# A macaron block of MoE FFN and Mamba: the FFN down projection as three f32r products, with its weight halves streamed

## The reference

```python
x = x + 0.5 * ffn(layernorm(x))        # call f1
x = x + attn(layernorm(x))             # Mamba block and gated MLP
x = x + 0.5 * ffn(layernorm(x))        # call f2, same weights

def ffn(x):                            # 32 experts of 96, top 6, shared 192
    scores = sigmoid(x @ gate_w); topk_w, topk_i = top_k(scores, 6)
    combine = one-hot sum of topk_w / sum(topk_w)
    act = silu(einsum('td,edf->tef', x, wg)) * einsum('td,edf->tef', x, wu)
    routed = einsum('tef,efd,te->td', act, wd, combine)
    return routed + (silu(x @ sg) * (x @ su)) @ sd

def attn(h):                           # d_inner 512, 16 states, conv 4
    h = h + mamba(rmsnorm(h))
    return h + mlp(rmsnorm(h))         # gated MLP, 1024 hidden
```

## Time and profile before

| | us |
|---|---|
| median of 3 runs | 1938.59 (1936.56 to 1942.36) |
| the profiled execution, its own time | 1936.02 |
| its span in the profile | 1934.2 |
| PE busy (matmuls) | 1601.1 (83%) |
| DVE busy | 1295.1 (67%) |
| POOL busy | 720.2 (37%) |
| ACT busy | 705.1 (36%) |

### The profile page before, as it was taken

How to read it: one execution, slowest core, us unless ns; L and a number is a source line. 1 busy time by engine, 2 the same in 40 slices (tenths; PEclk the granted TensorE clock), 3 DMA queues, 4 the chain that set the end, 5 groups by cost and what they waited for, 6 DMA issues and landing times. The chain is left out here.

```text
span 1934.2 us, 25234 instructions
## 1 busy us (share of the span) xinstructions
PE 1601.1 (83%) x7512; PEld 1194.2 (62%) x7512; DVE 1295.1 (67%) x2331; ACT 705.1 (36%) x1418; POOL 720.2 (37%) x838
## 2 busy tenths in 40 slices
PE   6776768677978988789888989788988998678999
PEld 5665557555755557455664557555675567556888
DVE  3236984688468964789466974689648974896343
ACT  4234424433352425333343423433244334432211
POOL 4411552244134532345223542245324542353222
PEclk9887889878999999899998999899999999988999
DMA  7752223323232222222231223222232223323563
GB/s 260 281 170 91 86 86 99 111 88 98 78 106 72 81 89 74 105 74 80 80 104 65 84 77 95 85 77 88 81 98 93 87 77 86 126 88 101 174 205 133
DMA packets 72751, 204.77 MB, mean 106 GB/s; under 512 B 12928, under 2 KB 22368, under 8 KB 72224
## 3 DMA queue, kind: packets, MB, share of 16 engines
q1 hardware_dynamic: 64416, 177.86, 27.7%
q0 software_dynamic: 8192, 25.17, 4.5%
HBM read 179.39 MB, written 15.73 MB: 101 GB/s over the span
## 5 line engine op out<-in xcount | busy, mean ns | idle before, releaser
L595 PE MATMUL gub<-x_hi,wr 128*128 128x256 f32 (+1 forms) x1144 | 460.5, 403 | 83.5 <-DVE hid L963 60.6
L675 PE MATMUL acc<-hid,w_down 128*128 128x256 f32 (+1 forms) x1144 | 423.9, 498 | 0.9 <-DVE hid L963 0.8
L1218 POOL TENSOR_TENSOR hid<-hid,weight 128x256 f32<-128x256 f32 (+1 forms) x264 | 263.5, 998 | 428.0 <-DVE hid L963 409.9
L824 ACT ACTIVATE hid<-gub 128x256 f32<-128x256 f32 (+1 forms) x350 | 160.9, 460 | 680.5 <-PE gub L597 590.5
L596 PE MATMUL gub<-x_lo,wr 128*128 128x256 f32 (+1 forms) x1144 | 395.7, 346 | 0.0
L597 PE MATMUL gub<-x_hi,wr 128*128 128x256 f32 (+1 forms) x1144 | 394.7, 345 | 0.0
L1231 POOL TENSOR_TENSOR ring<-ring 128x512 f32<-128x512 f32 x192 | 245.8, 1280 | 314.4 <-DVE ring L1118 314.4
L1112 DVE TENSOR_TENSOR_SCAN ring<-decays,side 128x512 f32<-128x512 f32 x256 | 310.7, 1214 | 4.1 <-DVE side L1103 1.5
L595 PEld LDWEIGHTS gub<-x_hi,wr 128*128 128x128 f32 x1144 | 231.9, 203 | 122.1 <-issue 73.9
L675 PEld LDWEIGHTS acc<-hid,w_down 128*128 128x128 f32 x1144 | 212.9, 201 | 88.3 <-issue 68.8
L596 PEld LDWEIGHTS gub<-x_lo,wr 128*128 128x128 f32 x1144 | 232.3, 203 | 21.1 <-issue 4.3
(11 more groups left out here) (115 smaller groups left out, 1725.4 us busy)
## 6 DMA issues: line engine op xcount, KB each, us to landing
wr<-w_halves SPq DMA_DIRECT2D x260, 512.0 KB, 3.3
wm_gu<-in_w_mlp POOLq DMA_DIRECT2D x64, 256.0 KB, 3.0
w_halves<-wr SPq DMA_DIRECT2D x26, 512.0 KB, 4.9
wm_down<-in_w_mlp POOLq DMA_DIRECT2D x64, 128.0 KB, 2.6
w_raw<-in_w_gu SPq DMA_DIRECT2D x26, 256.0 KB, 4.7
cst<-decays SPq DMA_DIRECT2D x192, 32.0 KB, 1.9
xin<-in_x SPq DMA_DIRECT2D x8, 256.0 KB, 3.4
x<-in_x SPq DMA_DIRECT2D x8, 256.0 KB, 2.6
```

The costliest lines, as they stand in the source:

```text
L595: mm(out, w[:, 0, half, k, :], x_hi[:, k, a:b], start=(k == 0), stop=False)
L675: last = mm(acc[k][:, a:b], w, h[:, a:b], start=(c == 0), stop=(c == (MLP_CHUNKS if mlp else FFN_CHUNKS) - 1))
L824: A(hid[c % HSLOTS][:, a:b], s.gub_of(it)[:, a:b], ACT.Tanh, scale=0.5).then_inc(sem["tanh_done"], 1)
L1218: nc.gpsimd.tensor_tensor(h, h, weight[c // 3 % CSLOTS][:, a:b], ALU.mult).then_inc(sem["weighted"], 1)
```

## The change

The down projection becomes three f32r products per output half, as gate and up are: high weights times high hidden values, high times low, low times high. For this the hidden values are split in a new item `hh`: ACT copies hid to f32r (`h_hi`), POOL subtracts (`h_lo`), four slots each. The down weights are no longer resident: each chunk's raw tile, weight slot and DRAM copy hold gate, up and down. In turn 0 the subtraction of `ws` moves from POOL to DVE. DLAG goes from 3 to 4, a weight slot is freed by `down` instead of `u`, and the reload items move to the position of that down. The diff, cut to its core:

```diff
-WSLOTS, MSLOTS, HSLOTS = 8, 3, 4
+WSLOTS, MSLOTS, HSLOTS, PSLOTS = 8, 3, 4, 4
...
+    "hh": {"hid_hi": 1, "hid_lo": 1},
...
-DLAG = 3
+DLAG = 4
...
+        out += [("hh", "ff", p - 2)] if 2 <= p <= FFN_CHUNKS + 1 else []
         out += [("down", "ff", p - DLAG)] if p >= DLAG else []
         out += [("by_g", "ff", p), ("u", "ff", p)] if now else []
+        used = p - DLAG
         if splits:
             out += [("keep_w", p)] if now else []
             out += [("raw", p + RAWS)] if p + RAWS < FFN_CHUNKS else []
             out += [("ws", p + WAHEAD)] if p + WAHEAD < FFN_CHUNKS else []
-        elif p + WSLOTS < FFN_CHUNKS:
-            out += [("wl", p + WSLOTS)]
-        if now and more and p == last_in(p % WSLOTS):
-            out += [("wln", p % WSLOTS)]
+        elif used >= 0 and used + WSLOTS < FFN_CHUNKS:
+            out += [("wl", used + WSLOTS)]
+        if more and used >= 0 and used == last_in(used % WSLOTS):
+            out += [("wln", used % WSLOTS)]
...
-        w_raw = [sb(f"w_raw{i}", [P, 2, KC, P]) for i in range(RAWS)]
-        w_down = sb("w_down", [P, FFN_CHUNKS, DM])
+        w_raw = [sb(f"w_raw{i}", [P, 3, KC, P]) for i in range(RAWS)]
...
-        wr = [sb(f"wr{i}", [P, 2, 2, KC, P], F32R) for i in range(WSLOTS)]
+        wr = [sb(f"wr{i}", [P, 2, 3, KC, P], F32R) for i in range(WSLOTS)]
...
+        h_hi = [sb(f"h_hi{i}", [P, 2 * SEQ], F32R) for i in range(PSLOTS)]
+        h_lo = [sb(f"h_lo{i}", [P, 2 * SEQ], F32R) for i in range(PSLOTS)]
...
-                    sp.dma_start(w_raw[c % RAWS][:], d["w_gu"][c]).then_inc(sem[f"w_raw{c % RAWS}"], 16)
-                    for i, (lo, hi) in enumerate(SLICES):
-                        if c == max(lo, RAWS - 1):
-                            ffn_slice(i)
+                    sp.dma_start(w_raw[c % RAWS][:], d["w_ffn"][c]).then_inc(sem[f"w_raw{c % RAWS}"], 16)
...
-                    sp.wait_ge(sem["u_filled"], s.count("u_filled", ("u", "ff", before), 1))
+                    sp.wait_ge(sem["down_done"], s.count("down_done", ("down", "ff", before), 1))
...
-                    h = hid[c % HSLOTS]
-                    for k in range(KC):
-                        w = wm_down[c % MSLOTS][:, k, :] if mlp else w_down[:, c, k * P:(k + 1) * P]
-                        last = mm(acc[k][:, a:b], w, h[:, a:b], start=(c == 0),
-                                  stop=(c == (MLP_CHUNKS if mlp else FFN_CHUNKS) - 1))
...
+                        w = wr[c % WSLOTS]
+                        hi, lo = h_hi[c % PSLOTS][:, a:b], h_lo[c % PSLOTS][:, a:b]
+                        for k in range(KC):
+                            mm(acc[k][:, a:b], w[:, 0, 2, k, :], hi, start=(c == 0), stop=False)
+                            mm(acc[k][:, a:b], w[:, 0, 2, k, :], lo, start=False, stop=False)
+                            last = mm(acc[k][:, a:b], w[:, 1, 2, k, :], hi, start=False,
+                                      stop=(c == FFN_CHUNKS - 1))
...
+                elif kind == "hh":
...
+                    if c >= PSLOTS:
+                        act.wait_ge(sem["down_done"], s.count("down_done", ("down", "ff", c - PSLOTS), 1))
...
+                    A(h_hi[c % PSLOTS][:, a:b], hid[c % HSLOTS][:, a:b], ACT.Copy).then_inc(sem["hid_hi"], 1)
...
+                if kind == "ws":
...
+                    v.tensor_tensor(w[:, 1], w_raw[it[1] % RAWS][:], w[:, 0].bitcast(F32),
+                                    ALU.subtract).then_inc(sem["w_split"], 1)
...
+                if it[0] == "hh":
...
+                    pool.wait_ge(sem["hid_hi"], s.count("hid_hi", it, 1))
+                    nc.gpsimd.tensor_tensor(h_lo[c % PSLOTS][:, a:b], hid[c % HSLOTS][:, a:b],
+                                            h_hi[c % PSLOTS][:, a:b].bitcast(F32),
+                                            ALU.subtract).then_inc(sem["hid_lo"], 1)
```

More of the change, by code:

```diff
@@ L656, in do @@
                         pe.wait_ge(sem["residual"], least)
-                    if not mlp and c < ROUTED:
-                        pe.wait_ge(sem["weighted"], s.count("weighted", ("by_comb", call, c), 1))
-                    else:
[L660 to L665, removed]
+                    if mlp:
+                        pe.wait_ge(sem["hidden"], s.count("hidden", ("gum", "mlp", c), 1))
+                    else:
+                        pe.wait_ge(sem["hid_lo"], s.count("hid_lo", ("hh", "ff", c), 1))
                     if mlp:
@@ L814, in do @@
                         sem["comb_copied"], 1)
+                elif kind == "hh":
+                    c = it[2]
+                    a, b = spans[s.n]
+                    if c < ROUTED:
+                        act.wait_ge(sem["weighted"], s.count("weighted", ("by_comb", "ff", c), 1))
+                    else:
+                        act.wait_ge(sem["hidden"], s.count("hidden", ("by_u", "ff", c), 1))
+                    if c >= PSLOTS:
+                        act.wait_ge(sem["down_done"], s.count("down_done", ("down", "ff", c - PSLOTS), 1))
+                    elif (least := s.prior("down_done")) is not None:
+                        act.wait_ge(sem["down_done"], least)
+                    A(h_hi[c % PSLOTS][:, a:b], hid[c % HSLOTS][:, a:b], ACT.Copy).then_inc(sem["hid_hi"], 1)
                 elif kind in ("g", "gum"):
@@ L819, in do @@
                     act.wait_ge(sem[filled], s.count(filled, it, 1))
-                    if (least := s.count("down_done", ("down",) + it[1:], 1,
-                                         back=HSLOTS if c >= 2 else 2)) is not None:
-                        act.wait_ge(sem["down_done"], least)
+                    if c >= HSLOTS and kind == "gum":
+                        act.wait_ge(sem["down_done"], s.count("down_done", ("down", "mlp", c - HSLOTS), 1))
+                    elif c >= HSLOTS:
+                        act.wait_ge(sem["hid_lo"], s.count("hid_lo", ("hh", "ff", c - HSLOTS), 1))
+                    elif kind == "g" and ("end", "mlp") in s.at:
+                        act.wait_ge(sem["down_done"], s.count("down_done", ("down", "mlp", MLP_CHUNKS - 1), 1))
+                    elif (least := s.prior("hid_lo")) is not None:
+                        act.wait_ge(sem["hid_lo"], least)
                     A(hid[c % HSLOTS][:, a:b], s.gub_of(it)[:, a:b], ACT.Tanh,
@@ L943, in do @@
                 kind = it[0]
-                if kind == "gum":
+                if kind == "ws":
+                    w = wr[it[1] % WSLOTS]
+                    dve.wait_ge(sem["w_hi"], s.count("w_hi", it, 1))
+                    v.tensor_tensor(w[:, 1], w_raw[it[1] % RAWS][:], w[:, 0].bitcast(F32),
+                                    ALU.subtract).then_inc(sem["w_split"], 1)
+                elif kind == "gum":
                     h, b = hid[it[2] % HSLOTS][:, 0:SEQ], s.gub_of(it)
@@ L1267, in columns @@
         return w.reshape(KC, P, FFN_CHUNKS, P).transpose(2, 1, 0, 3)
-    w_gu = np.stack([columns(g["ffn_wg"], g["ffn_sg"]), columns(g["ffn_wu"], g["ffn_su"])], axis=2)
-    down = feat(np.concatenate([by_quarter(g["ffn_wd"]), g["ffn_sd"],
-                                np.zeros((pad, DM), np.float32)]))
+    down = np.concatenate([by_quarter(g["ffn_wd"]), g["ffn_sd"], np.zeros((pad, DM), np.float32)])
+    w_ffn = np.stack([columns(g["ffn_wg"], g["ffn_sg"]), columns(g["ffn_wu"], g["ffn_su"]),
+                      down.reshape(FFN_CHUNKS, P, KC, P)], axis=2)
     def hidden_chunks(w):
@@ L1300 @@
     arrays = {
-        "x": xt, "w_gu": w_gu, "w_down": down, "w_mlp": w_mlp,
+        "x": xt, "w_ffn": w_ffn, "w_mlp": w_mlp,
         "w_router": feat(g["ffn_gate_w"]), "w_in": w_in, "w_dt": c(g["attn_dt_proj_w"].T),
```

24 lines of the change are left out of this document (11 added, 13 removed).

## The result

The changed kernel takes 1955.4 us in the median of 10 runs (1946.8 to 1966.4), the kernel before beside it 1938.6: a ratio of 1.0088, 95% interval 1.0062 to 1.0113, so 0.9% or 17 us slower. The profiled execution took 1951.2 us with a span of 1949.4. Forecast were 1941.0 in a range of 1915 to 1963, with "slower" as the likeliest of the three cases (0.41). The total came out 14 us above the forecast and inside the range. But the forecast meant 2.4 us more than before, and measured are 17, and almost no term of the sum did what it was put down for.

A forecast was written before the change was run, and what follows sets the result against it. The bound was taken to vary by stage: PE in turns 9 and 10, DVE in parts of turn 4, the weight feed early in turn 0. The terms +10 -15 -2 +12 +1 -3.6 gave +2.4, so 1941 us, range 1915 to 1963.

The forecast's parts named there:

- Start of turn 1, +10: End of turn 0: DMA-bound by larger weights, so turn 1's first chunk starts 10 us later; ends -2 and +24.
- the 38.4 MB: Turn 0: keeps, raw tiles, reloads and Mamba weights moved before slot 1 is back; 112 us at 343 GB/s.
- 125 as a bound for being wrong: Sign for turn 1's first chunk: expected near 133 us; a start before 125 or after 145 would be wrong.
- PE's gain in turns 3 to 7, -15: Down products at 512 columns: each chunk 0.34 us shorter, 3.0 us a turn arriving; ends 0 and -27 in all.
- under 178: Sign in turn 4's FFN stage: 181 to 183 us expected; under 178 means PE counted for more.
- the 64 records outside the two stretches: Turns 3 to 7: 64 of 104 down records (16 of 26 chunks) can gain, at most 5.4 us a turn.
- Turns 1, 2 and 8, -2: Shorter down products there: -0.7 us each, at most 3.9 each; ends 0 and -12 together.
- ScalarE and POOL, +12: Splitting hid delays work queued behind it, such as five norms and a turn's last sum: 1.5 us a turn; ends 0, 34.
- rival 3: In-order queues: a copy and a subtraction on the path at every norm, +34 instead of +12: 1963 us; chance 0.12.
- a few us over 16 routings: DVE's router tensor_scalar: slowed by a third more POOL time through shared SBUF interfaces; left in the upper end.
- The weights in turns 2 to 8, 0: Turns starting with the MLP: 768 KB per some 7 us is little for the DMA engines, so 0 us.
- Turns 9 and 10, +1 and -3.6: Last FFN turns: turn 9's -3.8 lost to loads, +1 for collisions; turn 10's loads done in time, -3.6 us.
- Rival 2: The feed: turns 0 and 9 run at the DMA engines' pace, larger rows at 303 GB/s, +23: 1962 us; chance 0.17.

The follow-up runs named there:

- turned slots: Changed kernel with slot placement turned by two places between turns 0 and 1 and between turns 9 and 10: 1951.8 us, ratio 1.0053.
- small copies: Changed kernel with ScalarE's copy and POOL's subtraction of hid cut to 8 columns from turn 1 on: 1925.3 us, ratio 0.9923.
- the run with nine items held back: Changed kernel with TAIL 9 instead of 6, the number of a turn's last heavy items held back in merge: 1976.7 us, ratio 1.0198.
- POOL's extra subtraction: Kernel before the change, with a POOL subtraction that nobody uses added behind each product of hid with its combine weight: 1949.0 us, ratio 1.0044.
- late reloads: Changed kernel, last four reloads of turns 1 to 8 moved into the next MLP stage, empty items in their places: 1925.5 us, ratio 0.9912.
- the late reloads and the turned slots: Changed kernel with both cures, and turn 9's last four reloads behind the gate products of turn 10's first four chunks: 1911.7 us, ratio 0.9850.

## Why the prediction was right in total and wrong in its parts

That the total fell into the range is luck: the terms below are off by up to 25 us, in both directions.

**Start of turn 1, +10: measured 0.** The mechanism held: the DMA share of turn 0 is 0.97, the 5.5 us rhythm of the earlier trace rows is gone, and the turn's start hangs on the 38.4 MB. The size was off: from the first keep at 21.3 to 122.0 the DMA engines moved 38.3 MB, 380 GB/s in the mean and not the 343 of the earlier trace rows, and the chunk started at 122.55, as before. The failed step is the rate, taken from a stretch of smaller transfers: from 30 to 65 us there were 3826 packets with 12.0 MB before the change and 3500 with 14.4 MB after it, both times at a share near 1. That the longer rows are the reason was not tested. I had given 125 as a bound for being wrong, and it is. And the start wasn't bound by bytes alone: the turned slots brought it to 114.53 at the same bytes.

**PE's gain in turns 3 to 7, -15: measured -28.** The FFN stages of turns 3 to 6 became 33 us shorter (8.3 each), with POOL's cost inside; my upper end was 5.4 a turn. Turn 7's became 5.5 longer. With small copies those of turns 3 to 6 became 56 us shorter, 14 each. The sign for it stood in the prediction: turn 4's stage took 173.0, under 178. The step that failed is counting only the 64 records outside the two stretches at DVE's pace. But all 26 chunks x 0.34 are 8.8 us a turn, less than those 14, so more than the products must be in it; the run with nine items held back shows that the order moves these four stages by 17 us, and I did not look at how new items shift merge. What the kernel before would do in the new order was not run, so how the 33 us divide between products and order stays open.

**Turns 1, 2 and 8, -2: measured +9** (0.7 for turns 0 and 1 together, 6.1 and 2.1). Why turn 2's FFN stage is longer stays open; it was 152 to 157 us in every variant of the changed kernel.

**ScalarE and POOL, +12: measured at least 26 for POOL's subtraction and some 6 for the copy.** That is near rival 3, whose price was 34 in all. The split of it was wrong: I counted ends of queues at five norms, and called POOL's effect on DVE a few us over 16 routings. The instruction of the earlier trace rows did rise by only 2.6 us in all with POOL's extra subtraction (532 to 692 ns in the mean), but it was not the only one of its kind: DVE's own busy time rose by 17 us.

**The weights in turns 2 to 8, 0: measured +25 in the MLP stages.** A term put at nothing, this is the step that, with POOL's subtraction, made the kernel slower. "768 KB per some 7 us is little" is true of the mean (114 GB/s in turn 4) and was read from a mean. The change's own rule, a slot freed by down, puts four reloads into the last 5 us of a turn. I had listed the transfer's lead (4 chunks instead of 8) and not when the last ones leave, nor what stands behind them at that moment: the store, the next sequence and the code behind the jump. Moving them away gave back 34 us (27 to 41, the two intervals taken together); some of that, as in turn 2, the change had not cost.

**Turns 9 and 10, +1 and -3.6: measured +4.0 and +4.7.** The FFN stage of turn 9 gained 1.4. Its MLP stage lost 5.4, of which the late reloads gave back 1.8; another 1.4 are the products at half clock behind PE's wait for POOL, and the rest is open. Turn 10 lost through its start, not its pace: 6.1 us for slot 0. The forecast of 59 us was 61.2 once the order was right. I had the last reload in at about 1873; it left at 1878.6 as the eighth in 10 us.

Rival 2, the feed, was right in that the weights cost most (the late reloads and the turned slots gave back 46 us together, the small copies 32), and wrong in the place: not the pace of turns 0 and 9, but the bursts at the turns' borders. The range held since PE's gain and the losses, each undersized, moved against each other.

## What to carry to other kernels

When a change moves the point that frees a buffer, list the transfers of the last few positions of a stage one by one, with their times, and ask what is queued behind them there; a mean rate can't show it. In this kernel, a transfer that is urgent for nobody should leave behind the stores and the jump of the border, and the slot that is needed first should be the one that is freed first. And an edit to a list that a merging rule spreads out changes the order of everything in it: an empty item in the old place separates the two effects, here 31 us.

## What the runs showed of the hardware

- 16 DMA engines moved 411 GB/s over 35 us (30 to 65 us of turn 0), reads and writes together, where before they moved 343 with a share of 0.99 as well. A share of 1 says that the engines are occupied, not at what rate. The Trainium skill (DMA: Bandwidth & Descriptors, Specifications) has 358 GB/s as the HBM limit of a core and 435 as the fabric's; with one core running, the trace lies above the first and below the second.
- A store of 256 KB that took 2.6 us at a border before the change took 6.1 us behind four reloads and held DVE for 9.1 us behind eight.
- Idle times of 3.2 and 3.4 us of PE were each followed by a granted clock of 0.50, over some 7 and 10 us; in turn 7 the 3.24 us of idling made the 16 products behind it 2.8 us longer. Idle times of 2.1 us (border into turn 9) and 1.4 us (border into turn 6 with late reloads) were followed by 0.50 for some 3 us, one of 1.5 us in the kernel before by none.
- POOL busy for 257 us more made DVE busy for 17 us more, on a few of its instructions alone (the one on xs 449 to 648 ns).
